# Attention in a fused two-layer kernel: values stationary, probabilities moving, row sums inverted by way of HBM

## The reference

```python
q = (h @ Wq).reshape(b, s, 16, 64);  k, v = (h @ Wk), (h @ Wv)   # 4 heads of keys and values, rotated q and k
p = softmax(causal(q @ k.T / 8))                                 # 1024 x 1024 a head, f32
out = (p @ v).reshape(b, s, 1024) @ Wo                           # 1024 x 256
x = x + gate * out
```

## Time and profile before

| | us |
|---|---|
| median of 3 runs (2279.39 to 2283.38) | 2281.24 |
| span of the profiled execution | 2273.4 |
| TensorE busy in it | 1949.5 (86%) |
| VectorE busy | 1369.2 (60%) |
| ScalarE busy | 854.9 (38%) |
| GpSimd busy | 488.5 (21%) |
| chain of work that ended last: TensorE / VectorE / ScalarE | 58% / 22% / 5% |
| of it the values' products, L447 | 20% |

### The profile page before, as it was taken

How to read it: one execution, slowest core, us unless ns; L and a number is a source line. 1 busy time by engine, 2 the same in 40 slices (tenths; PEclk the granted TensorE clock), 3 DMA queues, 4 the chain that set the end, 5 groups by cost and what they waited for, 6 DMA issues and landing times.

```text
span 2273.4 us, 32271 instructions
## 1 busy us (share of the span) xinstructions
PE 1949.5 (86%) x11764; PEld 1718.9 (76%) x11764; DVE 1369.2 (60%) x3130; ACT 854.9 (38%) x1697; POOL 488.5 (21%) x940
## 2 busy tenths in 40 slices
PE   6858799999875789999976779999987587999997
PEld 4637699999744779999864569999976476999886
DVE  4688565463668755554358865555445885555535
ACT  1403444543331344445232334454423034444523
POOL 0231222121123212221023222112112322222111
PEclk8979799999987889999987879999998798999999
DMA  5400000000410000000050000000031000000005
GB/s 206 176 0 1 1 1 2 1 1 1 167 48 0 1 1 2 1 1 1 6 208 1 1 1 2 1 1 1 2 149 65 0 1 1 2 1 1 1 1 185
DMA packets 28526, 70.80 MB, mean 31 GB/s; under 512 B 4607, under 2 KB 19775, under 8 KB 24774
## 3 DMA queue, kind: packets, MB, share of 16 engines
q1 hardware_dynamic: 28358, 68.60, 8.2%
HBM read 58.35 MB, written 9.98 MB: 30 GB/s over the span
## 4 chain that ended last, share of the span: by engine, by line
PE 58%; DVE 22%; ACT 5%; DVEq 5%; issue 5%; DMA 2%; POOL 1%; SPq 0%; POOLq 0%; ACTq 0%
PE ps L447 20%; PE ps L293 7%; DVE ps L950 6%; PE ps L597 5%; PE ps L434 4%; PE ps L416 4%; PE ps L433 4%; PE ps L299 3%; DVE prod L1012 3%; PE ps L620 3%; PE ps L395 2%; ACT qhh L683 2%; DVE hrow L856 2%; DMA gate_scratch<-grow 1%; DVEq L1020 1%
## 5 line engine op out<-in xcount | busy, mean ns | idle before, releaser
L447 PEld LDWEIGHTS ps<-v,pT 128*128 128x128 f32 x4608 | 546.0, 192 | 12.5 <-ACT pT L700 2.0
L447 PE MATMUL ps<-v,pT 128*128 128x65 f32 x4608 | 538.4, 272 | 1.5 <-ACT pT L700 1.5
L700 ACT ACTIVATE pT<-ps 128x512 f32<-128x512 f32 (+3 forms) x768 | 332.9, 492 | 344.6 <-PE ps L434 332.4
L950 DVE CUSTOM_DVE_ANT_0 ps<-ps,mrow 128x128 f32<-128x128 f32 (+7 forms) x512 | 373.0, 783 | 40.2 <-PE ps L416 40.2
L1152 POOL TENSOR_SCALAR_AFFINE_SELECT pT<-pT 128x128 f32<-128x128 f32 x512 | 146.0, 294 | 928.5 <-ACT pT L700 922.8
L433 PE MATMUL ps<-qhh,khl 128*128 128x512 f32 (+3 forms) x768 | 275.2, 362 | 9.2 <-DMA q<-nmr 9.2
L434 PE MATMUL ps<-q,k 65*128 65x512 f32 (+3 forms) x768 | 261.9, 354 | 0.0
L416 PE MATMUL ps<-khl,qhh 128*128 128x512 f32 (+3 forms) x768 | 230.0, 381 | 35.5 <-DVE mx L950 15.0
L659 ACT ACTIVATE hfull<-ps,modb 128x512 f32<-128x512 f32 x48 | 37.3, 777 | 455.8 <-PE ps L371 455.8
L960 DVE RECIPROCAL den<-ps 128x4 f32<-128x4 f32 x128 | 23.4, 183 | 299.8 <-PE ps L447 299.8
L943 DVE TENSOR_TENSOR q<-ps,qhh 64x512 fp32r<-64x512 f32 x128 | 87.4, 683 | 185.8 <-ACT qhh L683 185.8
(11 more groups left out here) (150 smaller groups left out, 2897.1 us busy)
## 6 DMA issues: line engine op xcount, KB each, us to landing
sgn<-sgn_scratch SPq DMA_DIRECT2D x8, 1024.0 KB, 13.4
Kf<-kf_scratch SPq DMA_DIRECT2D x4, 2048.0 KB, 17.6
in_w<-in_w_scratch SPq DMA_DIRECT2D x4, 1536.0 KB, 10.7
x<-in_x SPq DMA_DIRECT2D x5, 1024.0 KB, 5.9
xn<-in_x SPq DMA_DIRECT2D x4, 1024.0 KB, 7.5
out<-x SPq DMA_DIRECT2D x4, 1024.0 KB, 5.0
wraw<-in_wmod SPq DMA_DIRECT2D x2, 1536.0 KB, 6.7
fwd<-in_fwd SPq DMA_DIRECT2D x5, 512.0 KB, 18.4
```

The source lines that it names most:

```text
L447: q = mm(ps[:, b, (i % 4) * (HD + 1):(i % 4 + 1) * (HD + 1)], pT[:, slot, i * P - lo:(i + 1) * P - lo], v1[:, g % 2, j, :], start=j == 0, ...
L700: A(pT[:, n % PRING, 0:(c + 1) * HALF - lo], ps[:, b, 0:(c + 1) * HALF - lo], ACT.Exp, scale=SCALE)\
L950: V.tensor_tensor_reduce(out=v, in0=v, in1=mrow[:, L - n:L], scale=1.0, scalar=-3e38, op0=ALU.add, op1=ALU.max, accum_out=mx[:, u % 2, i:i ...
```

## The change

- `values(u, c, j)` now has `v1` of tile j as its stationary operand (128x65) and the probabilities of `score_cols(u, c, j)` as the moving one, up to 512 columns. 12 products a head; the result is 65 x 512, already turned, with the row sums as its row 64. `turn_outputs`, `normalise` and `orow` are gone.
- ScalarE copies each result to `osum` (`summed`; it lies over `hrow`). The sums of a head are then taken along: SP moves the row of 1024 sums to 128x8 (`den`), VectorE inverts it (`invert`), SP stores it to HBM, waits, and loads it back broadcast over 64 partitions (`rb`); VectorE multiplies `osum` by it into `oT` (`scale`). This happens in the next head: `invert(u - 1)` behind `turn_head(w)`, `scale(u - 1)` between row maxima 4 and 5. SP's three DMAs stand behind that of the head's maxima.
- PSUM banks go by purpose: 0 and 1 for the values, 2 and 3 for score columns, 4 to 7 for rows, turns and projections (4 and 6 for rows of two banks).
- TensorE's order in a head: columns of the first half; `turn_head(w)`; then columns of the second half, values of the first half, score rows and projection tiles in turn; for j = 4..7 column j, rows j, values j - 4 of the second half; values 4, `turn_maxima(w)`, values 5 to 7.
- The output projection starts with the seven pairs of heads that are ready for its first two banks and adds the last pair behind.

```diff
-            def values(u, c, i, b):
-                g = u // GQ
...
-                for j in range(i + 1):
...
-                    q = mm(ps[:, b, (i % 4) * (HD + 1):(i % 4 + 1) * (HD + 1)],
-                           pT[:, slot, i * P - lo:(i + 1) * P - lo], v1[:, g % 2, j, :],
-                           start=j == 0, stop=j == i)
+            def values(u, c, j):
+                g = u // GQ
+                if j == 0:
+                    sums[c] = bk.take(pe, ("pv", u, c), until=(s["o_done"], NHALF * u + c + 1), among=SUM_BANKS)
...
+                lo, hi = max(c * HALF, j * P), (c + 1) * HALF
+                if j * P >= c * HALF:
+                    pe.wait_ge(s["masked_done"], NT * u + j + 1)
+                else:
+                    pe.wait_ge(s["exp_done"], 12 * u + 4 * c + j + 1)
+                slot = (12 * u + 4 * c + j) % PRING
+                i = mm(ps[0:HD + 1, b, lo - c * HALF:HALF], v1[:, g % 2, j, :], pT[:, slot, 0:hi - lo],
+                       start=j == 0, stop=j == 4 * c + 3)
# TensorE, one head
                     for j in range(4):
                         score_cols(u, 0, j)
                     if w < HEADS:
                         turn_head(w)
-                    if u >= 2 and u % 2 == 0:
-                        turn_outputs(u // 2 - 1)
...
+                    score_cols(u, 1, 0)
...
+                    values(u, 0, 0)
...
+                    score_cols(u, 1, 1)
...
+                    values(u, 0, 1)
...
+                        score_rows(w, 0)
+                    score_cols(u, 1, 2)
+                    values(u, 0, 2)
+                        score_rows(w, 1)
+                    score_cols(u, 1, 3)
+                    values(u, 0, 3)
+                        score_rows(w, 2)
+                        score_rows(w, 3)
                     for j in range(4, NT):
                         score_cols(u, 1, j)
                         if w < HEADS:
                             score_rows(w, j)
+                        values(u, 1, j - 4)
+                    for j in range(4, NT):
+                        if j == 5 and w < HEADS:
+                            turn_maxima(w)
+                        values(u, 1, j)
# TensorE, output projection
+                pe.wait_ge(s["oT_done"], HEADS - 2)
+                first = [(t, bk.take(pe, ("out1", t))) for t in (0, 2)]
+                for t, b in first:
+                    for u in range(2):
+                        attended(t, u, b, range(HEADS // 2 - 1))
+                pe.wait_ge(s["oT_done"], HEADS)
# ScalarE
+            def summed(u, c):
+                b = bk.wait(act, ("pv", u, c))
+                if c == 0 and u >= 2:
+                    act.wait_ge(s["oT_done"], u - 1)
+                A(osum[:, u % 2, c * HALF:(c + 1) * HALF], ps[0:HD + 1, b, :], ACT.Copy).then_inc(s["o_done"], 1)
...
+                    if u:
+                        summed(u - 1, 1)
                     for j in range(4):
                         exps(u, 0, j)
                     if w < HEADS:
                         turn_head(w)
...
+                    exps(u, 1, 3)
+                    summed(u, 0)
+                    for j in range(4, NT):
                         exps(u, 1, j)
# VectorE
+            def invert(u):
+                dve.wait_ge(s["sum_loaded"], 16 * (u + 1))
...
+                V.reciprocal(rden[:, u % 2, :], den[:, u % 2, :]).then_inc(s["inverse_done"], 1)
+            def scale(u):
+                dve.wait_ge(s[f"inverse_loaded{u % 2}"], 16 * (u // 2 + 1))
+                V.tensor_tensor(oT[u % 2 * HD:(u % 2 + 1) * HD, u // 2, :], osum[0:HD, u % 2, :], rb[:, u % 2, :],
+                                ALU.mult).then_inc(s["oT_done"], 1)
...
                     if w < HEADS:
                         turn_head(w)
+                    if u:
+                        invert(u - 1)
                     if u % GQ == 2 and u // GQ + 1 < KV:
                         rotate(u // GQ + 1)
                     if w < HEADS:
-                        for i in range(3):
+                        for i in range(5):
                             row_maxima(w, i)
-                    normalise(u, 0)
+                    if u:
+                        scale(u - 1)
                     if w < HEADS:
-                        for i in range(3, NT):
+                        for i in range(5, NT):
                             row_maxima(w, i)
# SP, behind the DMA of the head's maxima
+                    if u:
+                        r = (u - 1) % 2
+                        sp.wait_ge(s["o_done"], NHALF * u)
+                        dma(den[:, r, :], osum[HD:HD + 1, r, :]).then_inc(s["sum_loaded"], 16)
+                        sp.wait_ge(s["inverse_done"], u)
+                        dma(inverse_scratch[r:r + 1, :].rearrange("a (p k) -> p (a k)", p=P), rden[:, r, :])\
+                            .then_inc(s["inverse_stored"], 16)
+                        sp.wait_ge(s["inverse_stored"], 16 * u)
+                        dma(rb[:, r, :], inverse_scratch[r:r + 1, :].broadcast_to([HD, L]))\
+                            .then_inc(s[f"inverse_loaded{r}"], 16)
```

More of the change, by code:

```diff
@@ L248, in reset, with take @@
                 self.at, self.uses, self.frees, self.owner, self.chunk = 0, [0] * 8, [0] * 8, [None] * 8, {}
[L250 to L254, removed]
+                self.turns = {}
+            def take(self, pe, key, n=1, until=None, among=None):
+                if among is None:
+                    while self.at % n:
+                        self.at += 1
+                    b = self.at % 8
+                    self.at += n
+                else:
+                    b = among[self.turns.get(among, 0) % len(among)]
+                    self.turns[among] = self.turns.get(among, 0) + 1
                 for q in range(b, b + n):
@@ L409, in score_rows @@
                 g, r, n = u // GQ, u % QRING, (i + 1) * P
-                b = bk.take(pe, ("rows", u, i), 1 if n <= HALF else 2)
+                b = bk.take(pe, ("rows", u, i), 1 if n <= HALF else 2, among=ROW_BANKS if n <= HALF else WIDE_BANKS)
                 if i % 4 == 0:
@@ L556, in _ @@
                 turn_maxima(0)
+                sums = {}
                 for u in range(HEADS):
@@ L582, in _, with attended @@
                             score_rows(w, j)
[L583 to L585 removed]
+                        values(u, 1, j - 4)
+                    for j in range(4, NT):
+                        if j == 5 and w < HEADS:
                             turn_maxima(w)
[L587 to L590 removed]
+                        values(u, 1, j)
+                def attended(t, u, b, some):
+                    for q in some:
+                        i = mm(ps[:, b, u * D:(u + 1) * D], oT[:, q, (t + u) * P:(t + u + 1) * P], wo[:, q, :],
+                               start=q == 0 and (u == 0 or t >= 4), stop=q == HEADS // 2 - 1 and (u == 1 or t >= 4))
+                    return i
+                pe.wait_ge(s["oT_done"], HEADS - 2)
[4 more added lines that the diff above has]
+                pe.wait_ge(s["oT_done"], HEADS)
+                for t, b in first:
+                    attended(t, 0, b, (HEADS // 2 - 1,))
+                    attended(t, 1, b, (HEADS // 2 - 1,)).then_inc(ready[b], 1)
+                for t in (4, 6):
                     b = bk.take(pe, ("out1", t))
[L592 removed]
                     for u in range(2):
@@ L595, in _ @@
                             route()
-                        for q in range(HEADS // 2):
-                            i = mm(ps[:, b, u * D:(u + 1) * D], oT[:, q, (t + u) * P:(t + u + 1) * P], wo[:, q, :],
-                                   start=q == 0, stop=q == HEADS // 2 - 1)
+                        i = attended(t, u, b, range(HEADS // 2))
                     i.then_inc(ready[b], 1)
@@ L758, in _ @@
                         turn_head(w)
-                    if u >= 2 and u % 2 == 0:
-                        turn_outputs(u // 2 - 1)
-                    if u % GQ == 2 and u // GQ + 1 < KV:
-                        value_rows(u // GQ + 1)
-                    for j in range(NT):
+                    following = u // GQ + 1 if u % GQ == 2 and u // GQ + 1 < KV else None
+                    if following:
+                        value_rows(following, range(0, 3))
+                    exps(u, 1, 0)
+                    if following:
+                        value_rows(following, range(3, 6))
+                    exps(u, 1, 1)
+                    if following:
+                        value_rows(following, range(6, 8))
+                    exps(u, 1, 2)
+                    exps(u, 1, 3)
+                    summed(u, 0)
+                    for j in range(4, NT):
                         exps(u, 1, j)
@@ L766, in _ @@
                         turn_maxima(w)
[L767 removed]
+                summed(HEADS - 1, 1)
                 for h in range(NHALF):
```

112 lines of the change are left out of this document (44 added, 68 removed).

## The result

The changed kernel takes 2395.77 us, median of 4 runs (2394.87 to 2403.27), against 2280.45 of the kernel before on the same chip: 1.051 times, 95% interval 1.049 to 1.053, so it is slower. The forecast was 2379, slower. The profiled execution spans 2392.8 us, 119.4 more than that of the kernel before (2273.4).

A forecast was written before the change was run, and what follows sets the result against it. TensorE bounds attention before the change; after it, the row sums' round trip through VectorE's order decides regular heads. 24.5 us a batch, 98 for four, take the span from 2273.4 to 2371; the median, 7.8 above, is 2379 (2350 to 2410).

The forecast's parts named there:

- The products with the values: TensorE's values products: fewer weights are loaded but moving columns cost the same, 7.83 us a head against 7.85, 0 gained.
- Transposes and the waits in the last rows: TensorE: output transposes go, 0.43 us a head, and waits for VectorE between last score rows go, 1.0: 1.4 gained.
- The seam: Between two heads: 3.7 us of TensorE work against the maxima chain's 5.1, a new wait of 1.4 us a head.
- Two column banks: Score columns wait for exponentials: 0.6 us at the head's start, 0.4 at the third column of the second half.
- The round trip: Row sums through HBM, store 2.2 and load 2.8 us, hold VectorE's scaling until 12.45; regular heads' period becomes 18.8 us.
- longer than 17.8, so this chain decides in regular heads: The round trip's period of 18.8 us exceeds 17.8, the period by TensorE and its seam and bank waits alone.
- rival (a): Round trip hidden, landings near 1.9 us, TensorE's own waits decide at 17.8 us a head: 2335; chance 0.20.
- Rival (d): Faster: seam and bank waits under 1.4 us, round trip under 3; regular heads 16.5: 2261; 0.11 including results toward 2335.
- Rival (c), the clock: Clock falls at the seams between heads, 1.2 us on the deciding chain each, 72 us more: 2450; chance 0.09.
- Sum: Per batch 8 regular heads x 2.0, keys 3 x 3.0, projection 3 x 0.3, head 0 0.3, end -1.8: 24.5 us.

The follow-up runs named there:

- all four edits: Changed kernel with scaling behind the negation, values 2 and 3 behind the last score rows, three column banks, another order of wide row banks: 2264.09 us, 0.993 times before.
- the second store: Changed kernel with the store of the inverted sums to HBM made twice, one behind the other: 2457.17 us, 1.078 times before.
- the kernel with four edits less one: Kernel with all four edits, but scaling stands between row maxima 4 and 5 again, as in the changed kernel: 2362.34 us, 1.037 times before.
- the kernel that scales last: Changed kernel with VectorE scaling the previous head's output behind its last row maximum and the negation: 2390.33 us, 1.049 times before.
- the other order of banks: The kernel that scales last, with wide score rows 4 taking first the bank pair in which rows 3 don't stand: 2353.88 us, 1.032 times before.
- the kernel with three column banks: Changed kernel with bank 1 given from the values to the score columns, leaving one values bank: 2355.72 us, 1.033 times before.
- the one whose seam was changed alone: Changed kernel with values 2 and 3 of the second half moved behind the last score rows, maxima turned ahead of values 4: 2367.73 us, 1.040 times before.
- those less the seam's: Kernel with all four edits, but values 2 and 3 stand between the last rows again: 2297.61 us, 1.008 times before.

## Why the prediction was right, point by point

*The products with the values* (forecast 0 gained, 7.83 us a head). Right. TensorE at the end of attention:

```profile
591.50 3.18 PE L461 MATMUL ps<-pT,v 128*65 128x512 f32 x10
594.51 20.89 PE L606 MATMUL ps<-wo,oT 128*128 128x256 f32 x96
```

10 records, 1792 columns, in 3.01 us: 1.68 ns a column for both records, 7.74 us a head. Weight loads of 65 columns and fewer of them bring nothing; the moving side is the price.

*Transposes and the waits in the last rows* (1.4 us a head gained). The sign was right, the size was not. It can be read only where the waits are gone: with all four edits a regular head takes 16.67 us on average, 0.5 of it idle ahead of the turn (30.5 us in 60 heads), so TensorE's part is near 16.2 and the gain 0.6, of which the transposes are 0.43. The wait for VectorE among the last rows was in the kernel before, a little smaller than the 1.0 taken:

```profile
366.39 0.28 PE L434 MATMUL ps<-q,k 65*128 65x256 f32 x1
366.93 0.64 PE L416 MATMUL ps<-khl,qhh 128*128 128x512 f32 x2 [0.27 <-DVE mx L950]
...
367.47 0.27 PE L434 MATMUL ps<-q,k 65*128 65x128 f32 x1
```

The next starts stand 0.54 and (367.85) 0.38 behind products of 256 and 128 columns, whose own price is 0.12 and 0.06: 0.74 us of waiting. With four edits it is gone, but other small waits have taken part of its place, 0.25 us ahead of the fourth column product among them; the rest was not followed up. The recorded working has a slip besides: 6400 columns in 2.7 to 3.1 us is a quarter of 1.70 ns a column, not half; half would be 5.4 us, more than the whole stretch of 3.96.

*The seam* (1.4 us). The chain was forecast at 5.1 us and is 5.03. The cover was forecast too small: TensorE idles 0.96 for the DMA and about 0.2 ahead of the turn. The runs didn't remove the whole wait. They moved cover: 0.9 us of it is worth 0.48 a head in the kernel with four edits, 1.5 us of it 0.67 in the kernel before. So 1.4 us as the price of the seam is not shown, and it was probably too high.

*Two column banks* (0.6 and 0.4). The starts at 1.45 and (5.25 + 0.4) 5.65 us into the head are 1.40 and 5.69. The worth of the third bank, the clock left out, is 0.45 a head in a kernel in which the round trip stands next to it; without the round trip it was not measured.

*The round trip* (12.45 us to the end of scaling, period 18.8). Store and load are each off, 1.4 for 2.2 and 3.4 for 2.8, and cancel: scaling begins 10.95 in for 11.15. Periods of 18.2 to 18.65 for 18.8, and 20.2 to 21.3 for 21.2 with keys. That it costs nearly its whole length is shown by the second store (61 us) and by the kernel with four edits less one (98 us).

The prediction weighed the Trainium skill's "DMA: Bandwidth & Descriptors" (Anatomy of one DMA), whose figures are fitted for DMAs that GpSimd issues; these are issued by SP. Its 2.0 us fixed, with HBM as the slowest target, is not what this store shows: 4 KB to HBM land in 1.4, less than 4 KB into this core's memory (2.0 for the sums' row). The load, 256 KB, took 3.4 where its figures give 2.6. Their sum, 4.6 against 4.8 measured, is near only because the two errors cancel.

*The step that failed* is a sentence in between: "longer than 17.8, so this chain decides in regular heads". TensorE's own limit is 17.7 in a quarter of the regular heads, 18.0 in another and 18.65 in half of them (the kernel that scales last); the 18.65 is through the row banks, as the run with the other order of banks shows. The prediction gave the four row banks no price. In that half the round trip did not decide. So rival (a), the round trip hidden, would have come out not at 2335 but near the 2390 of the kernel that scales last. That the total wasn't touched is luck: 18.65 happens to be close to 18.8.

*Rival (d)*, priced at 16.5 us a regular head, 17.9 with keys and 2261 in all, was on condition that the waits at the seam and at the banks are small. The four edits make that condition, and give 16.5 and 16.8, 17.9, and 2264.

*Rival (c), the clock*, was given 72 us if it came; it came in part. Windows of 4 us (TensorE's busy time, then granted clock behind the engines):

```profile
370.00:374.00 4.00, 2.69 (x18) 2.04 (x17) 0.00 (x0) 2.25 (x6) 1.03 (x4) 1.00 0.02 2
...
390.00:394.00 4.00, 3.67 (x18) 3.01 (x17) 0.00 (x0) 2.82 (x6) 1.17 (x4) 0.66 0.02 1
```

In the first of these seams the clock stays at 2.4 GHz; in the next, with the same waits of 0.96 and 0.33 us, it falls to 1.2 for part of the window. In the four batches 8 regular heads, one with keys and 4 with a projection were hit, 0.5 to 1.7 us each, 16 us, and two heads 0 took 1.6 longer: some 20 us of the 119. Behind the last copy of maxima it fell in two batches of four, 1.7 us each. The Trainium skill's "TensorE: Matmul & The Clock Gate" tells, in the part on PSUM-queue cycling behind HAM oscillation, of a kernel whose short idle times between groups of matmuls made the clock swing between the two levels. The trace agrees that it can fall without a long gap, though here it did so behind 15 of 60 seams only.

*Sum.* The terms for a batch were: regular heads +16.0, keys +9.0, projection +0.9, head 0 +0.3, end -1.8 (24.4, written as 24.5). Measured in the first batch: +15.5, +7.9, +6.0, +2.9, and -0.5 at the end, with the clock down in two heads with a projection, in head 0 and at the end (17.18 us from the last copy of maxima to the output projection, 17.67 before). Where the clock didn't fall, the means of the four batches are +13.4, +7.7, +2.8, +1.3 and -2.1 (15.52 us): 23 us a batch, 92 for four where 98 was forecast. Regular heads were priced too high (18.47 for 18.8), heads with a projection too low: head 6 loses 0.5 and not 0.3, heads 2 and 10 lose 1.1, 0.6 of which is the wait at the row banks. The fallen clock adds some 23 us, in the periods and at the end; this the prediction had left to rival (c), and it is why the spans differ by 119 and not by 98. A last piece of luck is in the total: the 7.8 us that lead from the span to the median compare two executions, for a run's own time lies only 2 us above its span (2394.87 for 2392.8). Without the other 6 us the forecast would have been near 2373.

## What to carry to other kernels

When an operation is moved so that TensorE's cost stays equal, the change is worth what its new waits leave: here four small edits of order and banks were worth 132 us, and only without those waits does the new form win, by 0.7% over a kernel before that got no such edits. A wait placed in an in-order engine costs whoever is queued behind it: put the use of a long round trip behind the last step that anyone waits for. And where several limits are nearly equal, removing one shows little (2 to 5 us here, against 61 for lengthening it and 98 for putting it back where the others are gone); test it by lengthening it, or in a kernel from which the others are gone.

## What wasn't expected of the hardware

- A store of 4 KB to HBM from 128 partitions, 32 bytes each, landed in 1.4 us at the median, faster than 4 KB from one partition to 128 within the core (2.0) and than 4 KB from 8 partitions into one (1.9).
- Behind the first head of a batch the clock fell in the changed kernel and in the four that keep its column banks and its seam (scaling last, two stores, both, the other order of row banks), 12 to 19 times in a profiled execution. It never fell in the kernel with three column banks, nor in the one whose seam was changed alone, nor in the one with all four edits; with those less the seam's it fell once. Of the two waits at the start of a head, 0.96 us for the maxima and 0.33 for the third column, either alone was thus followed by a fall at most once in 60 heads, both together by one in some heads. It also fell where VectorE's longer waits held the score rows (four edits less scaling last, 16 times). By what rule was not tried.
- Matmuls with 65 stationary columns cost per moving column what those with 128 do, 1.68 ns (1.70), as long as the moving side is the longer one; a third as many weight loads for the values saved no time.
